# A fused attention and mixture-of-experts kernel: ScalarE's jobs of a round in another order, expert weights and selectors prepared elsewhere on VectorE

## What is computed

```python
h = layernorm(x) * (1 + ca) + sa
wave = silu(h @ wave_w.T + wave_b)              # 16 columns: a frequency and a phase
kernel = silu(h @ kernel_w.T + kernel_b)        # 8 heads x 33 weights of samples
pos = clip(l + s * freq_avg + phase_avg, 0, 255)  # 33 places per row
out_h = sum over s of (h interpolated at pos) * kernel
x = x + ga * silu(out @ out_w.T)
h = layernorm(x) * (1 + cb) + sb
logits = h @ router_w.T + router_b
x = x + gb * (sum of the two best experts: h @ expert_w[e].T + expert_b[e])
```

## Time and profile before

| | |
|---|---|
| median of 3 runs | 292.21 us |
| time of the profiled execution | 291.6 us |
| its span (first to last instruction) | 289.8 us |
| busy: TensorE, VectorE, ScalarE, GpSimd | 263.6, 259.2, 228.0, 40.2 us |
| share of the span | 91%, 89%, 79%, 14% |
| mean granted TensorE clock | 0.988 of full speed |
| chain that ended last: ScalarE, VectorE, TensorE, issue | 32%, 31%, 24%, 11% |

### The profile page before, as it was taken

The page is one execution under the profiler, slowest core; times in us unless marked ns, Lnnn a source line. Parts: engine busy times, 40 slices in busy tenths (PEclk is TensorE's granted clock), DMA queues, the critical chain, the costliest instruction groups (busy, mean ns, idle before and its releaser), DMA issues.

```text
span 289.8 us, 5448 instructions
## 1 busy us (share of the span) xinstructions
PE 263.6 (91%) x1884; PEld 182.7 (63%) x1884; DVE 259.2 (89%) x543; ACT 228.0 (79%) x641; POOL 40.2 (14%) x61
## 2 busy tenths in 40 slices
PE   7999886999889998999899998999999989999895
PEld 3444642874567476866587477837884778487664
DVE  7989999998969998999989998999999999973462
ACT  4885899599978998899979998899779767655310
POOL 4203402300410022000200012002400300040100
PEclk9999998699999999999999999999999999999999
DMA  6550000020002000050005000500041004100101
GB/s 180 195 129 0 0 0 0 2 66 1 1 0 119 31 1 0 3 163 3 0 1 165 0 0 2 160 8 1 2 104 62 1 0 118 49 2 0 38 0 54
DMA packets 11869, 12.08 MB, mean 42 GB/s; under 512 B 1014, under 2 KB 10818, under 8 KB 11842
## 3 DMA queue, kind: packets, MB, share of 16 engines
q1 hardware_dynamic: 11398, 11.33, 13.0%
q10 hardware_dynamic: 444, 0.40, 0.5%
HBM read 9.59 MB, written 2.14 MB: 40 GB/s over the span
## 4 chain that ended last, share of the span: by engine, by line
ACT 32%; DVE 31%; PE 24%; issue 11%; POOL 1%; ACTq 0%; DVEq 0%; POOLq 0%
DVE AT L847 13%; ACT A L519 6%; DVE T L814 5%; ACT xn L383 4%; PE pT L1066 4%; ACT xn L417 4%; ACT c L502 3%; PE pE L1151 3%; PE pY L1151 2%; PE pL L1117 2%; PE pR L1066 2%; ACT u L484 2%; ACT T L453 2%; ACT hT L440 2%; PE pR L1043 1%
## 5 line engine op out<-in xcount | busy, mean ns | idle before, releaser
L814 DVE COPY_PREDICATED T<-mask,T 128x1472 f32<-128x1472 int16 (+9 forms) x54 | 76.6, 1418 | 0.5
L847 DVE TENSOR_TENSOR AT<-T,c 128x2064 f32<-128x2064 f32 x32 | 72.4, 2305 | 0.0
L519 ACT ACTIVATE A<-pT 128x512 f32<-128x512 f32 x64 | 35.1, 603 | 27.6 <-PE pT L1066 27.0
L1151 PE MATMUL pE<-hm,late 128*128 128x256 f32 x196 | 47.0, 387 | 0.0
L1151 PEld LDWEIGHTS pE<-hm,late 128*128 128x128 f32 x196 | 35.8, 190 | 5.9
L1066 PE MATMUL pT<-first,AT 128*128 128x128 f32 x256 | 34.6, 279 | 3.2 <-DVE AT L857 3.1
L519 ACT ACTIVATE A<-pR 128x512 f32<-128x512 f32 x64 | 35.5, 622 | 0.3 <-PE pR L1066 0.3
L322 POOL TENSOR_SCALAR ve<-sq 128x4 f32<-128x4 f32 (+1 forms) x14 | 9.9, 710 | 185.3 <-ACT xn L383 185.3
L1066 PEld LDWEIGHTS pT<-first,AT 128*128 128x128 f32 x256 | 29.4, 144 | 9.2 <-DVE AT L857 7.7
L1066 PE MATMUL pR<-first,AT 128*128 128x128 f32 x256 | 33.9, 276 | 0.0
L1080 PE MATMUL pY<-A,hs 128*32 128x256 f32 x512 | 32.4, 383 | 0.3
(11 more groups left out here) (153 smaller groups left out, 403.1 us busy)
## 6 DMA issues: line engine op xcount, KB each, us to landing
mkb<-mask_rows SPq DMA_DIRECT2D x6, 896.0 KB, 5.0
x<-in_x SPq DMA_DIRECT2D x7, 256.0 KB, 5.7
out<-x SPq DMA_DIRECT2D x7, 256.0 KB, 5.0
late<-in_late SPq DMA_DIRECT2D x1, 592.0 KB, 3.8
mkb<-mask_rows SPq DMA_DIRECT2D x1, 448.0 KB, 3.5
x<-in_x SPq DMA_DIRECT2D x2, 128.0 KB, 3.5
wmod<-in_wmod ACTq DMA_DIRECT2D x1, 256.0 KB, 4.4
out<-x SPq DMA_DIRECT2D x2, 128.0 KB, 3.2
```

The lines of the kernel that those rows point to most:

```text
L519: nc.scalar.activation(A[b][:, m, 2 * j:2 * j + 2, :].rearrange("p h l -> p (h l)"), four_banks(k)[:, :], ACT.Copy).then_inc(a_A, 1)
L814: nc.vector.copy_predicated(rows[:, :, :, j0:j1], spread(mask[:, k, 0:w, j0:j1], [P, w, H, j1 - j0], 2), rows[:, :, :, j0 + (1 << bit):j1 ...
L847: nc.vector.tensor_tensor(cells_of(bt).rearrange("p h (j r) -> p h j r", r=BLK), spread(T[n % 2][:, bt, 0:H, 0:NB], [P, H, NB, BLK], 3), s ...
L1151: ins = mm(dst, weT[:, e, :], hm[b][:, e, :], start=False, stop=(e == EM - 1))
```

## The change

On ScalarE four jobs change places in the round: `front_fall` goes from ahead of `front_row` 3 to behind `stats2`; `norm2` goes ahead of `sums1`; `back_h2T` goes ahead of `front_u` and `squares1`. `expert_weights` goes from GpSimd (round 0) to VectorE (round 1, ahead of `line`), and `selectors` from the end of VectorE's round 0 to ahead of `line` in that round. Since `h2T` is now overwritten sooner, TensorE takes the plain product and the biases for both images of a unit at once (`back_plain`, now 512 columns), and `back_x2T` goes into the second image's experts, after two of seven. The four warm-ups ahead of the logits stay in rounds 1 and 2 only.

```diff
@@ GpSimd
-            def expert_weights():
-                pool.wait_ge(d_late, 32)
-                nc.gpsimd.tensor_tensor(weT[:, 0:EM, :], weT[:, 0:EM, :], spread(weT[:, EM, :], [P, EM, C], 1),
-                                        ALU.subtract).then_inc(g_we, 1)
-                pool.wait_ge(g_we, 1)
-                nc.gpsimd.tensor_scalar(weT[:, EM, :], weT[:, EM, :], 2.0, None, ALU.mult).then_inc(g_we, 1)
...
-                if i == 0:
-                    expert_weights()
@@ ScalarE
                 run(i, 1, front_row, 2)
-                run(i, 0, front_fall)
                 run(i, 1, front_row, 3)
                 run(i, 1, front_wave)
...
                 run(i, -1, stats2)
+                run(i, 0, front_fall)
                 if i >= 0:
                     run(i, 1, front_hs)
+                run(i, -1, norm2)
                 run(i, 2, sums1)
+                run(i, -1, back_h2T)
                 run(i, 1, front_u)
-                run(i, -1, norm2)
                 if i < 0:
                     run(i, 1, front_hs)
                 run(i, 2, squares1)
-                run(i, -1, back_h2T)
                 run(i, -2, back_moe)
@@ VectorE
+            def expert_weights():
+                dve.wait_ge(d_late, 32)
+                nc.vector.tensor_tensor(weT[:, 0:EM, :], weT[:, 0:EM, :], spread(weT[:, EM, :], [P, EM, C], 1),
+                                        ALU.subtract).then_inc(v_we, 1)
+                dve.wait_ge(v_we, 1)
+                nc.vector.tensor_scalar(weT[:, EM, :], weT[:, EM, :], 2.0, None, ALU.mult).then_inc(v_we, 1)
...
                 run(i, 0, network, range(5, 6))
+                if i == 0:
+                    selectors()
+                elif i == 1:
+                    expert_weights()
                 run(i, 1, line)
...
                     gates()
-                    selectors()
@@ TensorE
             def back_experts(n, b, own=range(EM)):
                 img = before(n) + b
-                dst = moe_bank(n)[:, b * L:(b + 1) * L]
                 if own[0] == 0:
-                    back_plain(n, b, dst)
+                    if b == 0:
+                        back_plain(n)
+                    if n < LATE:
+                        pe.wait_ge(v_hm, img + 1)
...
+            def back_plain(n):
+                if n == 0:
+                    pe.wait_ge(v_ebp, 8)
+                    pe.wait_ge(v_we, 2)
...
+                pe.wait_ge(a_mk, n + 1)
+                w = tiles(n) * P
+                mm(moe_bank(n)[:, 0:w], weT[:, EM, :], h2T_of(n)[:, 0:w], start=True, stop=False)
+                mm(moe_bank(n)[:, 0:w], ebp[:, :], mkT_of(n)[:, 0:w], start=False, stop=False)
...
                 run(i, -2, back_experts, 0)
-                second(i, -2, back_experts, 1)
+                second(i, -2, back_experts, 1, range(0, 2))
...
                 run(i, -1, back_x2T)
-                if i > 0:
+                second(i, -2, back_experts, 1, range(2, EM))
+                if 0 < i < 3:
                     warm_up(4, pT[0])
                 run(i, -1, back_logits)
```

More of the change, by code:

```diff
@@ L185, in build @@
         a_mu2 = sem("a_mu2"); a_sq2 = sem("a_sq2"); g_ve2 = sem("g_ve2"); g_rs2 = sem("g_rs2"); a_xn2 = sem("a_xn2")
-        g_we = sem("g_we"); g_nm1 = sem("g_nm1"); g_nm2 = sem("g_nm2")
+        v_we = sem("v_we"); g_nm1 = sem("g_nm1"); g_nm2 = sem("g_nm2")
         t_xT = sem("t_xT"); a_hT = sem("a_hT"); t_hb = sem("t_hb"); a_hs = sem("a_hs")
@@ L1150, in back_experts @@
                         pe.wait_ge(v_hm, masked_before(img) + e // 2 + 1)
-                    ins = mm(dst, weT[:, e, :], hm[b][:, e, :], start=False, stop=(e == EM - 1))
+                    ins = mm(moe_bank(n)[:, b * L:(b + 1) * L], weT[:, e, :], hm[b][:, e, :], start=False,
+                             stop=(e == EM - 1 and b == UNITS[n][1] - 1))
                 if own[-1] == EM - 1:
                     ins.then_inc(t_moe, 1)
[L1155 to L1172, removed]
+            def back_plain(n):
+                if n == 0:
+                    pe.wait_ge(v_ebp, 8)
+                    pe.wait_ge(v_we, 2)
+                if n == LATE:
+                    pe.wait_ge(v_x2, NU)
+                elif n == LAST:
+                    pe.wait_ge(v_out, LATE)
+                elif n > 0:
+                    pe.wait_ge(v_out, n)
+                pe.wait_ge(a_mk, n + 1)
+                w = tiles(n) * P
+                mm(moe_bank(n)[:, 0:w], weT[:, EM, :], h2T_of(n)[:, 0:w], start=True, stop=False)
+                mm(moe_bank(n)[:, 0:w], ebp[:, :], mkT_of(n)[:, 0:w], start=False, stop=False)
             def back_out(n):
```

## The result

The changed kernel takes **295.02 us** (median of 6 runs, 294.61 to 297.75), the kernel before 292.15 in the same comparison (6 runs, 291.55 to 293.46): ratio 1.0103, 95% interval 1.0058 to 1.0148. It is about 1% slower where 288.4 was forecast, and outside the range. The profiled execution took 295.19 us, with a span of 293.3.

A forecast was written before the change was run, and what follows sets the result against it. VectorE, busy 29.81 us of a 31 us round, was taken as the bound. Gains of 0.85 + 1.15 + 0.92 + 0.92 = 3.84 took the profiled 291.6 to 287.8, 288.4 in the median's terms; range 286.8 to 290.7.

The forecast's parts named there:

- Squares1 and moe then end at 146.3: ScalarE in round 4: both jobs end at 146.3, where the A copies began at 146.91 before.
- rival 3: GpSimd's second-norm nm falls behind AT in every round, as in round 2: +8.9 us, so 301; chance 0.06.
- lg in rounds 3 to 5: VectorE's wait for the logits goes: 1.15 us gained in round 3, 0.92 each in rounds 4 and 5.
- uR's slack: Round 4: ScalarE writes uR at 143.77, VectorE asks at 144.14; 0.37 us to spare, 3.8 before.
- Rival 1: GpSimd's nm slips behind VectorE's prodN in rounds 3 to 5: 2.0 us given back, 290.4; chance 0.16.
- Round 2: The 2.83 us wait moves from lg to places; the round by itself gives -0.1 to +0.2, nothing.
- The head: Moved expert weights and selectors, plus row 3's order: round 2's lg 0.85 us earlier; ends 1.45 earlier, 1.1 later.
- No gap of the new round exceeds 1 us: TensorE: the four warm-ups dropped from round 3 on (0.9 us) cost nothing, no gap being above 1 us.
- Rounds 6 and 7: VectorE had no lg wait there before, so the gain was put at 0.
- Tail at 0: The second image's plain matmuls (about 0.7 us) move ahead and are saved behind: 0, ends -0.7 and +0.7.
- rival 2: TensorE's clock gives the head's bad end: 2.0 us given back, 290.4; chance 0.12.

The follow-up runs named there:

- e1: The changed kernel with VectorE waiting for GpSimd's first-norm factors ahead of the second AT pair in rounds 1 to 6; 291.64 us.
- e4: The kernel before with only the expert weights and selectors moved to VectorE's new places; 292.53 us.
- e5: The changed kernel with TensorE's x2T behind all experts again in round 7 alone, as before; 295.22 us.
- e16: The changed kernel with, in round 7, x2T behind all experts and the four warm-ups ahead of the logits again; 293.46 us.
- e6: The changed kernel with VectorE's wait for the first norm's factors (rounds 1 to 6) and x2T behind all experts in round 7; 292.34 us.
- e13: e6 with eight more warm-up matmuls in TensorE's idle time of round 1; 292.34 us.
- e9: e6 with the expert weights and selectors back where the kernel before had them; 293.36 us.
- e10: e5 with squares1 ahead of the places on ScalarE; 301.12 us.
- e15: e13 with the four warm-ups ahead of round 7's logits again; 290.94 us.
- e3: The changed kernel with ScalarE's order of before, TensorE's order and the head staying new; 294.85 us.

## Why the prediction was wrong

**The step that failed** is in the part on ScalarE's order, "Squares1 and moe then end at 146.3". The working went on to the A copies of the first image and stopped. Squares1 has another reader, GpSimd's `rs` and `nm` of the first norm, and behind them norm1 and the second image's copies. Its own numbers would have shown the danger: 146.3 less moe's 0.8 puts the squares' end at 145.5, rs (1.01) behind ve at about 145.9 to 146.9, nm after it; and the second AT pair, 0.92 ahead of its 147.79, starts at 146.87. The room of two microseconds of before (nm done at 145.64, AT at 147.79) was gone, on both sides at once. The lock was in the text, in round 2 and rival 3, but only for the second norm's `nm`; that norm got through in each of rounds 3 to 6. Measured instead: the first norm's `rs` took 6.13 us where 1.01 was taken for granted, norm1 waited 1.96 for it, and the residual waited 1.27 to 1.51 us in each of rounds 3 to 6, where the sum had 0.

Point by point:
- **lg in rounds 3 to 5: right.** No wait; the gain of 0.92 to 1.15 was made and given back one step later. Period 30.05 forecast, 31.40 measured, 30.13 without the residual's wait, 30.52 in e1.
- **uR's slack: right in kind.** 0.37 forecast, 0.03 in the trace (uR done 145.59, read 145.62): the statistics gained less than the 0.34 worked out. Rival 1 (nm behind prodN) didn't happen: nm 0.20.
- **Round 2: right in kind.** Wait at places 3.31 ("some 3"), lg without a wait behind it, and by itself the round lost 0.27, where -0.1 to +0.2 was forecast.
- **The head: terms right, total 0.36 instead of 0.85** ahead at round 3. Weights 1.27 start to start (1.2 forecast), line(2) 0.68 earlier (0.8), near back at 0.34. Its price doesn't hold from one execution to the next, since the clock's low stretch in round 1 does not (e4, e5). ScalarE's idle time ahead of row 3 was 0.50 (0.6), `u` started 15.49 behind the hT copy (15.5).
- **"No gap of the new round exceeds 1 us": wrong in round 7.** It was worked out for round 4 (0.59 at x2T there) and used for all. Round 7 had a gap of 2.93 at x2T in the changed kernel, ahead of the place where the dropped warm-ups had stood, so x2T's new place made it and not their absence. With x2T behind the experts 1.11 was left ahead of the logits; that one the warm-ups fill, and only with them back did the gain show in the median (e16).
- **Rounds 6 and 7 "had no wait, so 0": wrong.** +1.40 and +1.72. Round 6 pays the residual like the others. In round 7 the clock fell behind TensorE's hole.
- **Tail at 0:** 0.56 gained, within its ends.
- **Rival 3** had the right sign and the right mechanism on the wrong instruction, with 6 us too much; rival 2 put the clock's cost in the head; it came in round 7.

In sum at VectorE's starts: 3.84 forecast ahead, 3.5 behind at the end, a difference of 7.3: 0.5 up to round 3, 4.3 in rounds 3 to 5 (3.0 of gain given back and 1.3 more), 1.4 in round 6, 1.7 in round 7, less 0.6 in the tail.

## What to carry to other kernels

When a job on an in-order engine moves, follow every reader of every job behind it to the end, through the idle-looking engine too: 1 us of GpSimd work whose window shrinks from both sides costs the length of VectorE's work around it, and then a wait on the busy engine, placed so that the small work gets in first, is cheaper than none. What a gap on TensorE costs, and so what a filler is worth, is to be worked out for the worst round, not for the steady one. And where the medians hide a gain that the profiles show, look at how the single runs scatter, and compare the fastest ones too: here they showed that one of those gains isn't there in every run.

## What the runs showed of the hardware that was not expected

- A GpSimd instruction of 1.01 us that started at 147.80 ended at 153.93, after two 2.3 us VectorE instructions and `near`. It needn't be `rs`: in rounds 1 and 6 `nm`, 0.20 long elsewhere, fell behind the same run of VectorE's instructions and took 4.44 (at 53.64) and 5.19 (at 210.70), ending 0.1 behind `near`. In round 2 `nm` (75.62, 1.74 long) ended at 77.36, between the two ATs of the first pair. Why one slips in and the other doesn't stays open.
- VectorE's predicated copy also goes with a slower GpSimd instruction: `ve` took 1.62 beside the copy in round 7 (ending at 231.26, the copy at 231.25) and 0.95 in the kernel before (228.87 and 228.86), 0.19 in round 4. That it is the copy was not tried by itself.
- The same order of instructions with the same idle times ahead (1.11 at round 7's logits) left TensorE at 2.4 GHz in the profiles of e6 and e13 and dropped it to 1.2 GHz in those of e5, e9 and e10, with a tail of 47.4, 48.2 and 48.0 us against 46.6, so 0.8 to 1.6 longer. That the nine longer runs of e13 are such falls is argued from e15, where filling one hole left 13 of 14 runs at 291.91 or below, and not seen run by run: e13's mean clocks don't part them (0.992 in the three fastest, 0.981 to 0.994 in the others).
- A longer idle time isn't always followed by a fall: e3 waited 2.37 at x2T in rounds 3 to 5 and kept a granted clock of 1.00, and lost it behind 3.1 in round 7.
